# Wide attention rebuilt on half-row score tiles, and the first stage's order changed, in an eight-layer kernel on one core

## What is computed

```
sim[b,q,c] = n[b,q].w1 + ctx[b,c].w2 + (n[b,q]*ctx[b,c]).w3 + b_sim
a          = softmax over c of sim                 # per query
batch      = softmax over q of max over c of sim   # per batch item
HQ = a @ (context side),  F3 = n * HQ,  hc[b] = sum over q of batch[b,q] * n[b,q]
X += n @ Wqv0 + HQ @ Wqv1 + (n*HQ) @ Wqv2 + (n*hc) @ Wqv3 + b_qv
```

## Time and profile before

| what | value |
|---|---|
| median of 3 runs | 1583.4 us (1582.73 to 1584.68) |
| the profiled execution's own time | 1583.33 us |
| its span | 1581.5 us |
| PE busy | 1358.5 us, 86% of the span |
| DVE, ACT, POOL busy | 1072.2, 931.7, 902.1 us |
| first stage | from 0 to 83.8 us |
| wide attention, setup | 1080.4 to 1134.4 us |
| wide attention, token tiles and closing norm | 1134.4 to 1247.5 us |

### The profile page before, as it was taken

The page is one execution under the profiler, slowest core; times in us unless marked ns, Lnnn a source line. Parts: engine busy times, 40 slices in busy tenths (PEclk is TensorE's granted clock), DMA queues, the critical chain, the costliest instruction groups (busy, mean ns, idle before and its releaser), DMA issues. The chain is left out here.

```text
span 1581.5 us, 24419 instructions
## 1 busy us (share of the span) xinstructions
PE 1358.5 (86%) x7636; PEld 1054.7 (67%) x7636; DVE 1072.2 (68%) x2133; ACT 931.7 (59%) x1430; POOL 902.1 (57%) x628
## 2 busy tenths in 40 slices
PE   4769999889788887779669999997999539999998
PEld 4657777546465666746558887884888428787876
DVE  5554444389499999969756666775366666666665
ACT  1248887654487877557436665555566327555554
POOL 1518888610399999822037775662444218665655
PEclk9969999999699999899779999999999659999999
DMA  6021111000000000040034446442000124444442
GB/s 243 1 35 41 47 40 46 9 1 2 1 1 1 1 0 0 1 162 2 1 104 128 127 125 174 126 127 115 1 1 0 54 53 127 124 130 119 131 121 88
DMA packets 51555, 103.22 MB, mean 65 GB/s; under 512 B 6248, under 2 KB 10928, under 8 KB 49936
## 3 DMA queue, kind: packets, MB, share of 16 engines
q1 hardware_dynamic: 51472, 102.17, 21.3%
HBM read 99.99 MB, written 2.16 MB: 65 GB/s over the span
## 5 line engine op out<-in xcount | busy, mean ns | idle before, releaser
L1894 POOL TENSOR_TENSOR RA<-RW 128x1024 f32<-128x1024 f32 x128 | 246.7, 1965 | 89.8 <-ACT RW L1855 89.8
L879 ACT ACTIVATE PS<-PS 128x512 f32<-128x512 f32 (+1 forms) x260 | 151.2, 582 | 217.6 <-PE PS L597 216.9
L972 POOL TENSOR_TENSOR l3f_hid_rest<-RW,l3f_hid_high 128x512 fp32r<-128x512 f32 x132 | 170.4, 1291 | 143.8 <-ACT l3f_hid_high L871 143.8
L972 POOL TENSOR_TENSOR l2f_hid_rest<-RW,l2f_hid_high 128x512 fp32r<-128x512 f32 x128 | 165.4, 1292 | 137.2 <-ACT l2f_hid_high L871 135.9
L972 POOL TENSOR_TENSOR l0f_hid_rest<-RW,l0f_hid_high 128x512 fp32r<-128x512 f32 x128 | 165.2, 1292 | 77.1 <-ACT l0f_hid_high L871 69.9
L932 DVE TENSOR_TENSOR RW<-RW,PS 128x512 f32<-128x512 f32 (+1 forms) x260 | 178.7, 687 | 11.7 <-DVE RW L927 1.0
L1925 PE MATMUL PS<-identf,RA 128*128 128x128 f32 x1024 | 140.6, 290 | 36.5 <-DVE RA L1816 32.3
L1925 PEld LDWEIGHTS PS<-identf,RA 128*128 128x128 f32 x1024 | 120.0, 148 | 71.1 <-DVE RA L1816 67.1
L1816 DVE SCALAR_TENSOR_TENSOR RA<-RA,RW,PS 128x1024 f32<-128x1024 f32 x128 | 157.0, 1277 | 12.0 <-ACT PS L1861 11.4
L1861 ACT ACTIVATE PS<-RA 128x1024 f32<-128x1024 f32 x128 | 130.1, 1026 | 54.2 <-DVE RA L1816 51.9
L932 DVE TENSOR_TENSOR RW<-RD,PS 128x512 f32<-128x512 f32 x128 | 87.9, 687 | 107.6 <-ACT PS L879 98.8
(11 more groups left out here) (338 smaller groups left out, 3450.9 us busy)
## 6 DMA issues: line engine op xcount, KB each, us to landing
RD<-l2f_kept SPq DMA_DIRECT2D x128, 256.0 KB, 3.6
RB<-l3f_kept SPq DMA_DIRECT2D x128, 256.0 KB, 3.7
RD<-l0f_kept SPq DMA_DIRECT2D x32, 256.0 KB, 3.1
RA<-in_w SPq DMA_DIRECT2D x2, 2048.0 KB
RA<-in_wg SPq DMA_DIRECT2D x2, 1024.0 KB, 9.7
RA<-in_wu SPq DMA_DIRECT2D x2, 1024.0 KB, 11.7
RA<-in_wd SPq DMA_DIRECT2D x2, 1024.0 KB, 13.6
RC<-in_wg SPq DMA_DIRECT2D x1, 2048.0 KB, 8.0
```

Of the source, the lines that this page charges most:

```text
L879: act.activation(gate, gate, e.func, bias=st.bias).then_inc(e.acted, 1)
L972: pool.tensor_tensor(rest, hid, high, ALU.subtract).then_inc(e.hidden_ready, 1)
L1894: pool.tensor_tensor(*pair_scores(r, h), ALU.add).then_inc(added, 1)
```

## The change

In the first stage:

- R and w2b are made between the variance and the reciprocal of the standard deviation, inside the norm (`between`); cols counts on the keys' semaphore.
- `Rests` is gone; the split runs through `Pieces` and `Split` in six spans. Two early spans of W1 (1024 columns each) are rounded by ACT right behind the norm, as soon as W1 has landed (`w1_loaded`), and subtracted by DVE ahead of the similarity chain. Four later spans are rounded by ACT and subtracted by POOL, two after `a_ready` (the normalised similarities), two after `w14_ready`.
- PE runs dummy matmuls of the identity (`keep_busy`) into a bank that is written later: 16 at the start, 10 after the similarity matmuls, 22 after the maxima's transposes.
- The similarity matmuls wait for each block of XT instead of for all; AT is turned and stored by block; ctxK's products come ahead of hc, F3 ahead of w14; the output's HQ and F3 matmuls of a block come ahead of its w14 matmuls.

In wide attention:

- V and K products alternate on PE ahead of the norm's transposes, and ACT stores both with bias. Masked keys, spread values and the head mask are gone.
- Scores are 16 matmuls of 64 rows (one head each) by 64 keys a tile, the two heads of a chunk in two row groups and two banks.
- `fold` makes VW with 16 matmuls of 64 rows into 64 output rows; ACT stores even batch items, DVE odd ones.
- The loop over tiles is written out; the order of each engine's jobs in a step is as before.

```
+            keep_busy(pe, k, HC, 16)
             norm_tensor(pe, k, nm)
             pe.wait_ge(w_ready, 1)
-            pe.wait_ge(nm.xt_ready, NB)
             for t in range(NT):
                 b = t // 2
+                if t % TPB == 0:
+                    pe.wait_ge(nm.xt_ready, t // TPB + 1)
                 pe.matmul(sim_ps[:, t, :], k.XT[:, bass.ts(t, P)], R[:, bass.ts(b, C)], start=True, stop=False)
                 mm = pe.matmul(sim_ps[:, t, :], w2b, k.ctxT[:, bass.ts(b, C)], start=False, stop=True)
             mm.then_inc(sim_ready, 1)
+            keep_busy(pe, k, HC, 10)
...
+def keep_busy(pe, k, bank, times):
+    for _ in range(times):
+        pe.matmul(k.PS[:, bank, 0:P], k.identf[:], k.identf[:], start=True, stop=True)
...
+            norm_vector(dve, k, nm, own, loaded=k.x_loaded, between=similarity_weights)
+            for m, span in enumerate(early_spans):
+                early.subtract(dve, m, span)
...
+            pool.wait_ge(a_ready, 1)
+            for m in range(2):
+                later.subtract(pool, m, later_spans[m])
+            pool.wait_ge(w14_ready, B)
+            for m in range(2, 4):
+                later.subtract(pool, m, later_spans[m])
...
+                for t in tiles:
+                    pe.matmul(o[t % TPB], HQ[:, bass.ts(t, P)], k.Wqv[:, 1, :], start=(t % TPB == 0), stop=False,
+                              skip_group_check=True)
+                    pe.matmul(o[t % TPB], F3[:, bass.ts(t, P)], k.Wqv[:, 2, :], start=False, stop=False,
+                              skip_group_check=True)
+                pe.wait_ge(w14_ready, 2 * q + 2)
+                for t in tiles:
+                    mm = pe.matmul(o[t % TPB], k.XT[:, bass.ts(t, P)], w14[:, t // 2, :], start=False, stop=True,
+                                   skip_group_check=True)
```

```
+            def scores(t):
+                b = t // 2
+                if t >= 2:
+                    pe.wait_ge(shifted, t - 1)
+                for c in range(8):
+                    pe.wait_ge(q_stored, b * JOBS + c // 2 + 1)
+                    for h in range(2):
+                        rows = slice(64 * h, 64 * h + 64)
+                        mm = pe.matmul(score[t % 2][:, BLK * h + C * c:BLK * h + C * (c + 1)],
+                                       QT[b % 2][rows, c, bass.ts(t % 2, P)], KT[rows, c, bass.ts(b, C)],
+                                       start=True, stop=True)
+                mm.then_inc(score_ready, 1)
+
+            def fold(b):
+                if b >= 2:
+                    pe.wait_ge(vw_stored[b % 2], b // 2)
+                for jj in range(4):
+                    for h in range(2):
+                        for half in range(2):
+                            rows, j, c = slice(64 * h, 64 * h + 64), 4 * h + jj, 2 * jj + half
+                            mm = pe.matmul(vw_ps[b % 2][64 * half:64 * half + 64, bass.ts(j, D)],
+                                           VT[rows, c, bass.ts(b, C)], wo[rows, c, :], start=True, stop=True)
+                mm.then_inc(vw_ready, 1)
...
+            pe.wait_ge(nm.xt_ready, NB)
+            fold(0)
+            scores(0)
+            scores(1)
+            pe.wait_ge(q_stored, JOBS)
+            for b in range(1, B):
+                fold(b)
...
+                if t < 2:
+                    for b in ((1,), (3, 5, 7))[t]:
+                        dve.wait_ge(vw_ready, b + 1)
+                        dve.tensor_copy(VW[:, b].rearrange("p j d -> p (j d)"), vw_ps[1]).then_inc(vw_stored[1], 1)
```

More of the change, by code:

```diff
@@ L396, in constants, with __init__, cut, pair @@
                                   pattern=[[1, G3], [-1, G3]], channel_multiplier=0))
+class Pieces:
+    def __init__(self, k, name, region, at, pieces, rows=P):
+        self.pieces = []
+        for n, (width, rest_region, rest_at) in enumerate(pieces):
+            self.pieces.append((k.region[region][0:rows, at:at + width],
+                                k.rounded(f"{name}_high{n}", region, at, width, rows),
+                                k.rounded(f"{name}_rest{n}", rest_region, rest_at, width, rows)))
+            at += width
+    def cut(self, at, width):
+        for piece in self.pieces:
+            if at < piece[0].shape[1]:
+                return tuple(a[:, at:at + width] for a in piece)
+            at -= piece[0].shape[1]
+    def pair(self, at, width=P):
+        return self.cut(at, width)[1:]
+class Split:
+    def __init__(self, k, name):
+        self.rounded, self.subtracted = k.sem(f"{name}_rounded"), k.sem(f"{name}_subtracted")
+        self.ready, self.paced = k.sem(f"{name}_parts_split"), k.sem(f"{name}_paced")
+    def round(self, act, span):
+        whole, high, rest = span
+        act.activation(rest, whole, ACT.Copy).then_inc(self.rounded, 1)
+    def subtract(self, pool, n, span):
+        whole, high, rest = span
+        pool.wait_ge(self.rounded, n + 1)
+        pool.sem_inc(self.paced, 1)
+        pool.tensor_tensor(rest, whole, rest, ALU.subtract).then_inc(self.subtracted, 1)
+    def finish(self, act, n, span):
+        whole, high, rest = span
+        act.wait_ge(self.subtracted, n + 1)
+        act.sem_inc(self.paced, 1)
+        act.activation(high, whole, ACT.Copy).then_inc(self.ready, 1)
+def keep_busy(pe, k, bank, times):
+    for _ in range(times):
+        pe.matmul(k.PS[:, bank, 0:P], k.identf[:], k.identf[:], start=True, stop=True)
 def similarity_attention(k):
@@ L405, in similarity_attention @@
     n, fit = E0 * F0, (E0 - 1) * F0
-    split = k.l0f_split = Rests(k, "l0f_w", [("RA", 0, n, "RB", 10496, P), ("RA", n, fit, "RA", 8448, P),
-                                             ("RA", n + fit, F0, "RB", 10496 + n, P)])
+    w1 = Pieces(k, "l0f_w1", "RA", 0, [(n, "RB", 10496)])
+    w2 = Pieces(k, "l0f_w2", "RA", n, [(fit, "RA", 8448), (F0, "RB", 10496 + n)])
+    k.l0f_weights = (w1, w2)
+    early, later = Split(k, "l0f_early"), Split(k, "l0f_later")
+    early_spans = [w1.cut(0, 1024), w1.cut(1024, 1024)]
+    later_spans = [w1.cut(2048, 2048), w2.cut(0, 2048), w2.cut(2048, fit - 2048), w2.cut(fit, F0)]
     vec, gps = k.sem("l0x_vector"), k.sem("l0x_gpsimd")
@@ L515, in _ @@
             norm_scalar(act, k, nm)
+            act.wait_ge(k.w1_loaded, 16)
+            for span in early_spans:
+                early.round(act, span)
             act.wait_ge(shifted, 1)
@@ L551, in _ @@
             mm.then_inc(bc_turned, 1)
+            pe.wait_ge(k.l0x_loaded, 32)
+            for b in range(B):
+                pe.wait_ge(at_ready, b // 2 + 1)
+                mm = pe.matmul(PS[:, b // 2, bass.ts(b % 2, S)], k.ctxK[:, b, :], AT[:, bass.ts(b, S)],
+                               start=True, stop=True)
+                if b % 2:
+                    mm.then_inc(hq_done, 1)
             pe.wait_ge(bc_ready, 1)
@@ L1075, in gelu_experts @@
     nm, r = SplitNorm(k, "l0f", k.X, "RB", 8320, counted=True), Route(k, "l0f", E0, 1)
-    w1, w2, w2_last = (part[1:] for part in k.l0f_split.parts)
-    fit = (E0 - 1) * F0
-    chunk = lambda pair, c: tuple(a[:, bass.ts(c, P)] for a in pair)
-    last = fit // P
-    steps = [Step(chunk(w1, c), None, chunk(w2, c) if c < last else chunk(w2_last, c - last),
-                  bias=k.col("b1_0", c), spread=(c // K0, 1), fresh=(c % K0 == 0))
+    w1, w2 = k.l0f_weights
+    steps = [Step(w1.pair(c * P), None, w2.pair(c * P), bias=k.col("b1_0", c), spread=(c // K0, 1),
+                  fresh=(c % K0 == 0))
              for c in range(E0 * K0)]
@@ L2079, in attention_3 @@
[L2079 to L2082 removed]
+    nc, PS, RA, RB, RW = k.nc, k.PS, k.RA, k.RB, k.RW
+    nm, post = Norm(k, "l3x", k.X, counted=True), PostNorm(k)
+    s = lambda what: k.sem(f"l3x_{what}")
+    vec, biased = s("vector"), s("biased")
+    v_ready, v_stored, k_ready, k_stored = s("v_ready"), s("v_stored"), s("k_ready"), s("k_stored")
```

646 lines of the change are left out of this document (224 added, 422 removed).

## The result

The changed kernel takes **1540.7 us** (median of 4 runs, 1538.8 to 1546.8) against 1583.5 in runs beside it: a ratio of 0.9736, interval 0.9706 to 0.9765. The forecast was 1545, in 1537 to 1556. The profiled execution took 1538.8, which is 44.5 less than that of before. Its span is 1537.1.

The account below looks back on a forecast made before the run. No engine was taken to set the pace throughout; layers run one after another, so each change counts in its own stage. 1583.3 - 27 (first stage) - 11.5 (wide attention) = 1544.8, forecast 1545 us, range 1537 to 1556 (8 in 10).

Parts of the forecast that it names:

- The first stage: -27: First stage: 10.8 us gained up to the similarity chain's start, some 16 behind it; 28 gained, taken 27, bounds 24 to 30.
- the new last arrival: First stage: DVE's early W1 subtractions end at 21.2, 0.4 past the similarity matmuls, so the similarity chain starts at 21.3.
- Keep-busy matmuls: First stage: 16 dummies at the start put the similarity matmuls at 2.4 GHz, half of 13.9 us, so 6.9 gained.
- the 4.2 that the prediction gave it: First stage: with R and w2b moved into DVE's wait, similarity matmuls start at about 13.9, 4.2 us earlier.
- The first rival: First stage: the clock isn't kept and similarity matmuls run at the lower level again; +7, 1552 us; chance 20%.
- The second rival: First stage: POOL's subtraction precedes DVE's batch-weight scaling, so batch transposes and context products wait 4.5 us; 1549.5; chance 10%.
- Wide attention's setup: Setup up to tile 2's scores, which end at 1124 instead of 1136.4: 12.4 us gained, taken 11.5, bounds 7 to 14.
- scores may grow by that free: Token tiles: 0.3 to 0.4 us of PE waiting covers longer scores; priced at 0, dear side 0.1 a tile.
- The third rival: Token tiles: mode changes drain TensorE, 1.1 us a tile, 0.75 beyond the cover; +10.5 over 14 tiles, 1555.5; chance 8%.
- The row that the prediction read for it: Another attention stage: two 64-row matmuls took 1.13 us, 0.27 above 0.86 without a gap, read as a possible mode-change price.
- The fourth rival: Token tiles: half-row matmuls do not overlap, 5.1 us for 1.8, +3.2 a tile beyond the cover; +45, 1590; chance 3%.
- Their work is unchanged: Gelu experts only read the same weight pieces under new names; priced at nothing.

Follow-up runs that it names:

- the gap run: The changed kernel, dummies kept, but PE waits for POOL's bias addition before the similarity matmuls; 1553.7 us (1551.3 to 1555.3).
- The run with q ahead: The changed kernel with the first q job of each tile step ahead of the scores instead of behind them; median 1541.7 us.

## Why the prediction was right, point by point

- **The total** is near by the sum of its parts, and a little by luck: the two edited stages are 37.9 shorter in the first pair of profiles (forecast 38.5), which alone gives 1545.5. The other 6.5 that made it 1538.8 came from stages with unchanged work, and the changed kernel's second measurement is 1548.1.
- **The first stage: -27, measured -27.96.** The sum held at nearly each point: chain start 21.3 (21.48), chain end 29.0 (29.16), context products to 35.1 (34.95), hc to 39.4 (40.12), last output 52.7 (52.77). The last of these agrees because errors cancel: hc took 5.17 up to the output for the 4.3 in the sum, the output 12.65 for 13.3. The early subtraction, named as the new last arrival, ended 0.6 before the similarity matmuls did, which were 0.6 later than forecast. The end of this stage differs by 3.7 between profiles of one program, so an agreement within 1 is also luck.
- **"*Keep-busy matmuls* ... What they give: the similarity matmuls at 2.4 GHz"** is right for the changed kernel: its clock comes up in the dummies and stays. The 6.9 that it gives are 6.6 (from 13.9 to 7.3). But the sum books them to the dummies alone, and these are neither enough nor shown to be needed. With the dummies and the gap the level is lost, and the chain starts 11.1 later: 4.5 for the later start of the matmuls, 6.6 for their pace. Without the dummies and without the gap it came in the one execution profiled, with 0.8 to spare; how often the transposes alone bring the clock up was not counted. So moving R and w2b ahead of the normalisation carried more than the 4.2 that the prediction gave it. The first rival's price of 7 is near the 6.6 of the gap run; the pauses that it feared between the transposes were there (16 in 4.18, where the later stage's take 1.91) and did not cost the level.
- **The second rival's mechanism is real, its place was right, and its price too low:** 7.6 for 4.5. The wait is 2.67, shorter than priced; the rest comes from the clock, which falls right behind it (granted 0.67 from 34 to 36, 0.50 up to 50). It didn't happen, by 0.11 us. The 4.43 of the scaling is what the Trainium skill (SBUF — State Buffer, Who interferes with whom) says of the second to issue: blocked until the first is done.
- **Wide attention's setup: 12.4 worked out, 11.94 measured**, and its links hold: products done after 16.8 (16.9), q(1) started after 38.10 (38.1), tile 2's scores done after 44.05 (43.6).
- **The token tiles: "scores may grow by that free" was wrong.** The 0.3 to 0.4 of waiting stands behind the transposes, but scores lie ahead of a q job whose store ACT was about to begin with only 0.10 to spare. The scores' block costs 0.24 a tile more, so the period grew by 0.14: 1.4 over ten periods, and with 0.4 in the last tiles and 0.2 ahead of the first copy the 2.03. The rule of the Trainium skill (TensorEngine Tiling (Array Packing), Key Properties: changing the mode drains TensorE) agrees with these 0.24, which lie at the block's two ends; that it is the drain and nothing else about such a block, no run separates. The run with q ahead shows that it was a matter of place. The third rival had the mechanism; it priced it more than four times too high. The row that the prediction read for it does not bear on it: four full-size passes of q, with no change of mode, take the same 1.13 for the same pace of 0.86, since a group's duration includes the end of its last pass.
- **The fourth rival, no overlap,** did not occur; forced by the order of two loops it costs 36 and the change's whole gain. That this is near the 45 given is luck: the scores took 3.39 and not 5.1, as their passes followed each other by 0.11, without the load that the price added to each, and the falling clock made up for it. The rival's own terms, 5.1 for 1.8 with 0.3 to 0.4 covered, give 2.9 to 3.0 a tile and 41, not 3.2 and 45. That the two row groups overlap is shown: 32 passes take 1.93 up to the next matmul in one order, 3.32 in the other, at the same granted clock.
- **"Their work is unchanged", for all other stages,** holds for work and not for time. Product keys take 279.1 to 282.9 in the profiles, grouped experts 331.6 to 334.3, of kernels that are the same there; before had high values of both, the changed kernel's first profile low ones, its second high ones (282.87 and 333.6). So 5 of the 44.5 between the two profiled executions are no more than one program's own spread, and the bound of 3 us for what a measurement tells was too tight: medians of the same kernel were 1540.7 and 1548.1.

## What to carry to other kernels

Where matmuls are added to bring TensorE's clock up, look also for the gap behind them in which it falls again: with the dummies in place, a gap of 4.35 us cost itself and 6.6 more in the matmuls behind it. Free time on an engine inside a loop is no allowance for work ahead of another step in that loop: the slack of a place is what its own consumer waits beyond it, here 0.10 and not 0.4, and moving the growing step behind that consumer brought the period back to 6.70. And of these half-row matmuls, neighbours had to lie in different row groups: with one group after the other the whole gain of the change was gone.

## What the runs showed of the hardware that was not expected

- Similarity matmuls that start at 2.4 GHz stay there for 7 us; the same matmuls started at 1.2 GHz stayed there for 13.9 us (in the kernel before, where the clock had not yet come up, and with the gap kept, where it had and fell). Output matmuls did rise, after 3.5 us in the changed kernel.
- The clock's changes fall at other places in different executions of one program (the output reached 2.4 GHz at 43.67 in one, at 46.27 in another): the first stage of the same code ended between 53.83 and 57.52 in six profiles.
- A block of 64-row scores costs 0.10 at its beginning and 0.14 up to the next full-size matmul more than a block of full-size ones. Inside it a pair follows the pair before by 0.11, as single full-size passes do.
- An operation of 8 partitions by 256 columns on DVE, 0.34 long, is held 4.43 by a POOL subtraction that began 0.53 before it.
